# Attention scores in a Perceiver block: split fp32r products on the whole TensorE array, or full fp32 products on eight tiles of it

## The reference, cut to what matters

```python
q = (x @ Wq).reshape(B, N, H, D).transpose(0, 2, 1, 3)   # B 32, N 32, H 8, D 64
kv = (context @ Wkv).reshape(B, M, 2, H, D)              # M 257
k = kv[:, :, 0].transpose(0, 2, 1, 3)
v = kv[:, :, 1].transpose(0, 2, 1, 3)
q, k = _per_head_ln(q, qn_w), _per_head_ln(k, kn_w)
attn = jnp.einsum('bhnd,bhmd->bhnm', q, k) * SCALE       # the scores
attn = jnp.where(mask[:, None, :, :], attn, -jnp.inf)
attn = jax.nn.softmax(attn, axis=-1)
out = jnp.einsum('bhnm,bhmd->bhnd', attn, v)
```

## Time and profile before

| | |
|---|---|
| median of the three executions | 787.98 us |
| the profiled execution | 791.38 us |
| its span, first to last instruction | 789.6 us |
| mean granted clock of TensorE | 0.977 |
| PE busy, share of the span | 95% |
| steady batches, from 77 to 469 us | 392 us |

### The profile page before, as it was taken

One profiled execution on the slowest core, in us unless ns is written; L12 is line 12 of the kernel. 1 busy time (PEld: TensorE's weight loads), 2 busy tenths in 40 slices (PEclk: granted clock), 3 DMA queues, 4 the chain that ended last, 5 costly groups with the idle time before them and its releaser, 6 DMA issues.

```text
span 789.6 us, 13562 instructions
## 1 busy us (share of the span) xinstructions
PE 748.8 (95%) x4501; PEld 653.6 (83%) x4501; DVE 552.7 (70%) x1046; ACT 494.8 (63%) x1089; POOL 238.8 (30%) x182
## 2 busy tenths in 40 slices
PE   4898999999999999999999998999999958999996
PEld 3687899899999898998999997988788856877875
DVE  6877886776867868867868776885567754555573
ACT  4666786785867768767858666556465423655650
POOL 2562212121211212121212113842860002555545
PEclk9999999999999999999999999999999957999999
DMA  8841211212121211212121302661106472566658
GB/s 299 86 120 41 66 57 41 81 48 72 40 80 40 80 40 58 61 40 80 41 79 41 112 22 52 178 211 54 54 1 214 145 284 78 96 110 109 106 77 319
DMA packets 59671, 75.18 MB, mean 95 GB/s; under 512 B 8784, under 2 KB 33360, under 8 KB 59632
## 3 DMA queue, kind: packets, MB, share of 16 engines
q1 hardware_dynamic: 52032, 58.16, 24.8%
q0 software_dynamic: 4720, 11.27, 7.9%
q10 hardware_dynamic: 2880, 5.24, 1.8%
HBM read 54.75 MB, written 19.92 MB: 95 GB/s over the span
## 4 chain that ended last, share of the span: by engine, by line
PE 83%; DVE 7%; DMA 3%; ACT 3%; issue 2%; POOL 1%; SPq 0%; POOLq 0%; ACTq 0%; DVEq 0%
PE pK L32 38%; PE pV L32 14%; PE pP L32 11%; PE pS L32 6%; PE pT L1700 3%; PE pT L1519 3%; PE pP L1683 2%; DMA big<-x_rows,idx_x 1%; PE pT L1814 1%; DMA fin<-total 1%; PE pT L1499 1%; PE pS L1768 1%; DVE bst L976 1%; DMA total<-big,idx 1%; DVE head_mean L996 1%
## 5 line engine op out<-in xcount | busy, mean ns | idle before, releaser
L32 PE MATMUL pK<-parts 128*128 128x512 f32 x840 | 210.5, 398 | 0.7 <-POOL parts L547 0.7
L516 POOL TENSOR_TENSOR parts<-big,parts 128x1024 fp32r<-128x1024 f32 x32 | 77.3, 2416 | 338.8 <-ACT parts L741 338.8
L32 PEld LDWEIGHTS pK<-parts 128*128 128x128 f32 x840 | 152.3, 189 | 29.2 <-POOL parts L547 1.1
L32 PE MATMUL pK<-w,lhs 128*128 x276 | 71.5, 410 | 1.8 <-DVE lhs L1436 1.4
L32 PEld LDWEIGHTS pK<-w,lhs 128*128 128x128 f32 x276 | 51.9, 194 | 13.5 <-issue 3.5
L1018 DVE TENSOR_TENSOR kn<-pK,head_rs 128x512 f32<-128x512 f32 x62 | 42.6, 688 | 20.1 <-ACT head_rs L643 19.5
L1452 DVE TENSOR_TENSOR w_p<-big,w_p 128x1024 fp32r<-128x1024 f32 x22 | 27.0, 1226 | 39.5 <-ACT w_p L933 39.5
L769 ACT ACTIVATE pT<-pP 128x512 fp32r<-128x512 f32 x32 | 19.1, 598 | 55.6 <-PE pP L1683 55.6
L32 PE MATMUL pS<-kT,qblk 128*128 128x258 f32 x384 | 51.4, 284 | 2.0 <-DVE qoT L1052 2.0
L32 PE MATMUL pP<-pT,parts 128*128 128x256 f32 x384 | 53.0, 288 | 0.0
L32 PEld LDWEIGHTS pP<-pT,parts 128*128 128x128 f32 x384 | 47.6, 192 | 3.5
(11 more groups left out here) (320 smaller groups left out, 1638.2 us busy)
## 6 DMA issues: line engine op xcount, KB each, us to landing
big<-in_ctx_dram SPq DMA_DIRECT2D x32, 512.0 KB, 3.8
total<-zero SPq DMA_DIRECT2D x32, 256.0 KB, 4.0
w_raw<-in_L_ffn_w_dram SPq DMA_DIRECT2D x16, 512.0 KB, 5.6
big<-in_L_ffn_w_dram SPq DMA_DIRECT2D x8, 512.0 KB, 7.6
fin<-total SPq DMA_DIRECT2D x8, 512.0 KB, 7.2
big<-in_L_xattn_Wkv_dram SPq DMA_DIRECT2D x2, 1024.0 KB, 11.0
x_rows<-big ACTq DMA_DIRECT2D x8, 256.0 KB, 2.1
total<-big ACTq DMA_DIRECT2D x8, 256.0 KB, 2.4
```

The lines of the kernel that those rows point to most:

```text
L32: last = pe.matmul(out, lhs(a, c), rhs(b, c), start=start and c == first and n == 0, stop=stop and c == chunks - 1 and n == 2)
L516: nc.gpsimd.tensor_tensor(ctxN[:, u, LO], ctx_raw[:, u], ctxN[:, u, HI].bitcast(F32), ALU.subtract).then_inc(cn_lo, 1)
```

## The change

The queries and the keys of the scores are kept in fp32, unsplit. For each sequence POOL copies the queries into a compact tile `q_b` (one copy), ACT copies the keys of `pTT[0]` and DVE those of `pTT[1]` (one copy each). The scores of each head are one full fp32 product on a tile of the array of 64 rows by 32 columns, at `tile_position=(e * 64, c * 32)`: the stationary operand is the queries of the head (64 by 32), the moving operand its 257 keys. Head 2c+e writes rows 32c to 32c+31 of bank e, so the eight heads have eight different tiles. The order of the heads in the softmax tiles becomes (e, c), and `out_tile` reads its operands through `heads_of`, two pieces of 128 columns with a step between them. PE waits, ahead of the eight products, for five semaphores and a no-operation instruction. The zeroing of `qblk` and of a column of `kT` is dropped.

```diff
-        kT = at("kT", [P, 2, C, M + 1], 96 * KB, F32R)
-        qblk = at("qblk", [P, 2, 2, G, 3 * HD], 96 * KB + 8256, F32R)
+        kT = at("kT", [P, C, M], 96 * KB)
+        q_b = at("q_b", [P, 2, C, S], 96 * KB + 8256)
...
+        heads_of = lambda ap, c: ap.rearrange("p (e c) n -> p c e n", e=2)[:, c]
...
-            nc.gpsimd.memset(kT[:, :, :, M:M + 1].bitcast(F32), 0.0)
-            nc.gpsimd.memset(qblk[:, :, :, :, :].bitcast(F32), 0.0)
...
+            def queries(b, u, used=True):
+                if used:
+                    pool.wait_ge(sc_mm, b - 1)
+                nc.gpsimd.tensor_copy(q_b[:, u], qoT[:, :, bass.ds(b * S, S)]).then_inc(q_set, 1)
+
             ctx_parts(0, 0)
             low_part("xv", (2, 3))
+            pool.wait_ge(q_out, 1)
+            for b in range(2):
+                queries(b, b, used=False)
             ctx_parts(1, 1)
...
                 for u in range(2):
                     b = k * 2 + u
+                    queries(b, u)
                     ctx_parts(b, u)
...
+            def keys_copy(n):
+                act.wait_ge(k_t, (n - 1) * MT + 1)
+                act.activation(kT[:, :, 0:P], pTT[0][:, :, :], ACT.Copy).then_inc(kT0_set, 1)
...
                 if nxt:
-                    act.wait_ge(sc_mm, b)
-                    query_high(b + 1, 1 - u)
                     ctx_high(b + 1, 1 - u)
...
                 if main:
-                    for t in range(MT):
-                        act.wait_ge(k_t, b * MT + t + 1)
-                        act.activation(kT[:, HI, :, t * P:(t + 1) * P], pTT[t][:, :, :], ACT.Copy).then_inc(k_hi, 1)
+                    keys_copy(b + 1)
...
+            def keys_copy(n):
+                dve.wait_ge(k_t, n * MT)
+                ts(kT[:, :, P:MT * P], pTT[1][:, :, :], 1.0, None, ALU.mult).then_inc(kT1_set, 1)
...
                 if t == TILES - 1:
-                    query_low(1, 1)
+                    keys_copy(1)
                     dve.wait_ge(rem_act, 5)
-                    tt(kT_rem[:, LO], pAV[0][:, :, 0:B], kT_rem[:, HI].bitcast(F32), ALU.subtract).then_inc(rem_dve, 1)
-                    for n in range(MT):
-                        dve.wait_ge(k_hi, n + 1)
-                        tt(kT[:, LO, :, n * P:(n + 1) * P], pTT[n][:, :, :],
-                           kT[:, HI, :, n * P:(n + 1) * P].bitcast(F32), ALU.subtract).then_inc(k_lo, 1)
...
                 if nxt:
                     ctx_low(b + 1, 1 - u)
-                if nxt:
-                    query_low(b + 1, 1 - u)
...
                 if prev:
-                    pe.wait_ge(k_lo, b * MT)
-                    pe.wait_ge(qb_lo, b * 2)
+                    pe.wait_ge(kT0_set, b)
+                    pe.wait_ge(kT1_set, b)
                     pe.wait_ge(k_rem, b)
-                    for g in range(G):
-                        for j in range(2):
-                            c = 2 * g + j
-                            qb = lambda s, _: qblk[:, 1 - u, s, g, j * HD:j * HD + P]
-                            last = split_products(pe, pS[:, g, 0:M + 1], qb, lambda s, _: kT[:, s, c, :], 1,
-                                                  start=j == 0, stop=j == 1)
+                    pe.wait_ge(q_set, b)
+                    if not first:
+                        pe.wait_ge(sc_m, b - 1)
+                    pe.nop(nofuse=True)
+                    for c in range(C):
+                        for e in range(2):
+                            half = slice(e * HD, (e + 1) * HD)
+                            last = pe.matmul(pS[c * S:(c + 1) * S, e, 0:M], q_b[half, 1 - u, c, :],
+                                             kT[half, c, :], start=True, stop=True, tile_position=(e * HD, c * S))
                     last.then_inc(sc_mm, 1)
```

More of the change, by code:

```diff
@@ L164, in perceiver_block @@
         p_rem = at("p_rem", [P, G, 3, B], 117 * KB + 8320)
-        kT_rem = at("kT_rem", [P, 2, C, B], 118 * KB + 8064, F32R)
+        kT_rem = at("kT_rem", [P, C, B], 118 * KB + 8064)
         zero = at("zero", [P, P], 119 * KB + 8064)
@@ L265, in perceiver_block @@
         ctx_t, ctx_hi, ctx_lo = sem("ctx_t"), sem("ctx_hi"), sem("ctx_lo")
-        k_mm, k_sq, k_ss, k_lg, k_rs, k_n, k_t, k_hi, k_lo, k_rem = (sem(n) for n in (
-            "k_mm", "k_sq", "k_ss", "k_lg", "k_rs", "k_n", "k_t", "k_hi", "k_lo", "k_rem"))
+        k_mm, k_sq, k_ss, k_lg, k_rs, k_n, k_t, kT0_set, kT1_set, k_rem = (sem(n) for n in (
+            "k_mm", "k_sq", "k_ss", "k_lg", "k_rs", "k_n", "k_t", "kT0_set", "kT1_set", "k_rem"))
         cn_hi, cn_lo = sem("cn_hi"), sem("cn_lo")
         pc_mm, pc_hi, pc_lo = sem("pc_mm"), sem("pc_hi"), sem("pc_lo")
-        qb_hi, qb_lo, p_rs, p_rx, sel_set = (sem(n) for n in ("qb_hi", "qb_lo", "p_rs", "p_rx", "sel_set"))
+        q_set, p_rs, p_rx, sel_set = (sem(n) for n in ("q_set", "p_rs", "p_rx", "sel_set"))
         sc_mm, sc_m, sc_max, sc_exp, sc_step, p_n = (sem(n) for n in (
@@ L540, in _ @@
                     b = k * 2 + u
+                    queries(b, u)
                     ctx_parts(b, u)
-            ctx_parts(B - 2, 0)
-            ctx_parts(B - 1, 1)
+            for b in (B - 2, B - 1):
+                queries(b, b % 2)
+                ctx_parts(b, b % 2)
             def out_low(t):
@@ L662, in _ @@
             ln_scale(2)
-            def query_high(b, u):
-                for e in range(2):
-                    act.activation(q_half(b, u, HI, e), q_of(b, e), ACT.Copy).then_inc(qb_hi, 1)
             for t in range(TILES):
@@ L723, in _ @@
                     act.activation(head_rs[:, 2], head_log[:, 2], ACT.Exp, scale=-0.5).then_inc(k_rs, 1)
-                if t == 6:
-                    query_high(1, 1)
                 if t == TILES - 1:
@@ L728, in _ @@
                     act.wait_ge(rem_pe, 3)
-                    act.activation(kT_rem[:, HI], pAV[0][:, :, 0:B], ACT.Copy).then_inc(rem_act, 1)
-                    for n in range(MT):
-                        act.wait_ge(k_t, n + 1)
-                        act.activation(kT[:, HI, :, n * P:(n + 1) * P], pTT[n][:, :, :], ACT.Copy).then_inc(k_hi, 1)
+                    act.activation(kT_rem[:, :, :], pAV[0][:, :, 0:B], ACT.Copy).then_inc(rem_act, 1)
+                    keys_copy(1)
             k_square(1, 0)
@@ L1112, in _ @@
                 if t == TILES - 1:
-                    query_low(1, 1)
+                    keys_copy(1)
                     dve.wait_ge(rem_act, 5)
-                    tt(kT_rem[:, LO], pAV[0][:, :, 0:B], kT_rem[:, HI].bitcast(F32), ALU.subtract).then_inc(rem_dve, 1)
-                    for n in range(MT):
-                        dve.wait_ge(k_hi, n + 1)
-                        tt(kT[:, LO, :, n * P:(n + 1) * P], pTT[n][:, :, :],
-                           kT[:, HI, :, n * P:(n + 1) * P].bitcast(F32), ALU.subtract).then_inc(k_lo, 1)
-                    dve.wait_ge(rem_dve, 4)
-                    ts(kT[:, :, :, M - 1:M], kT_rem[:, :, :, 0:1].bitcast(F32), 1.0, None, ALU.mult).then_inc(k_rem, 1)
+                    ts(kT[:, :, M - 1:M], kT_rem[:, :, 0:1], 1.0, None, ALU.mult).then_inc(k_rem, 1)
             query_out(TILES - 1)
@@ L1188, in batch @@
                     dve.wait_ge(k_t, b * MT + 1)
[L1189 to L1193, removed]
+                    ts(kT[:, :, M - 1:M], kT_rem[:, :, bass.ds(b, 1)], 1.0, None, ALU.mult).then_inc(k_rem, 1)
+                    keys_copy(b + 1)
                 if main and not nxt:
@@ L1605, in out_tile @@
                     split_products(pe, o, lambda s, k: wkv[:, s, k, D + c * P:D + (c + 1) * P],
-                                   lambda s, k: z_p[:, s, k, c * 2 * P:(c + 1) * 2 * P], C, stop=False)
+                                   lambda s, k: heads_of(z_p[:, s, k].rearrange("p (h n) -> p h n", h=H), c), C, stop=False)
                     if c == 0:
@@ L1609, in out_tile @@
                     last = pe.matmul(o, vrem[0:3 * B, c * P:(c + 1) * P],
-                                     rem_b[0:3 * B, 2 * c:2 * c + 2].rearrange("p h b q -> p (h b q)"), start=False, stop=True)
+                                     heads_of(rem_b[0:3 * B].rearrange("p h b q -> p h (b q)"), c), start=False, stop=True)
                     if c % 2:
@@ L1675, in batch @@
                     if first:
-                        pe.wait_ge(rem_dve, 4)
+                        pe.wait_ge(rem_act, 5)
                     else:
@@ L1710, in batch @@
                                 if first:
-                                    pe.wait_ge(rem_dve, 5)
+                                    pe.wait_ge(rem_dve, 4)
                                 elif r == 0:
```

8 lines of the change are left out of this document (removed).

## The result

The changed kernel takes 766.85 us (median of four, 766.68 to 767.52) against 788.31 us for the kernel before in the same comparison: 21.5 us less, a ratio of 0.973 with a 95% interval of 0.9713 to 0.9747. The forecast was faster by 3.8 us, with a range that ended at 770: the side was right, the size was not, and the result lies outside the range.

A forecast was written before the change was run, and what follows sets the result against it. PE was taken to bound the loop: 2.9 us saved in the scores over 32 sequences and 0.9 us once at the start, 788.0 - 3.8 = 784.2 us; own range 770 to 793, for all cases 770 to 816.

The forecast's parts named there:

- The new waits: PE's added waits for the score copy, key copies and query copies: all met ahead of need, costing nothing.
- The start: Chain through DVE ahead of the first scores: they start near 63.4 in place of 64.34, saving 0.9 us once.
- The two ends: Entering and leaving the tiled shape on PE: 0 to 0.56 us together, taken at the middle, 0.28 us.
- the emptied array: Rival: PE empties at both shape changes around the scores, paying the full 0.56 us; 793 us, chance 0.13.
- the body of X: PE time of the sixteen tile passes of a sequence's scores, without the entry and exit cost: 1.07 us.
- X: PE time from scores' start to transposes' start: 1.35 us, range 0.9 to 1.63, against 1.44 before; 2.9 us saved.
- 14 issues at 0.05 us: Score passes limited by issue: last tile's first pass starts at 0.70 us, the scores' passes take 1.12 us.
- five passes in a row: Each half of the rows works its four tiles in order, neighbouring tiles' passes overlapping: 5 x 0.213 = 1.07 us.
- The lower end: Bound for the score passes on PE: all eight tiles at once, two passes, 2 x 0.213 = 0.43 us.
- One order for all tiles: Rival: score matmuls start in program order, only one pass overlapping the next tile's; X 2.2 us, 811 us, chance 0.21.
- no overlap: Rival: the score tiles run one after the other, X 3.7 us; 859 us, chance 0.09.
- The hidden gain: Rival: PE's scores get shorter, but PE then waits for the probabilities; 787 us, chance 0.07.

The follow-up runs named there:

- the work put back: Changed kernel with copies and subtractions into unused memory on ACT and DVE, about the work they had lost: 768.0 us, ratio 0.9736.
- the run with the halves apart: Changed kernel with the four tiles of the upper half of the rows issued first, then the four of the lower half: 767.52 us, ratio 0.9742.
- the run with each head twice: Changed kernel with each head's product issued twice in a row on its tile, same output: 781.53 us, ratio 0.9904.

## Why the prediction was wrong in size

**Right.** PE alone bounds the loop, and everything of ACT, DVE and POOL in it is under its cover: the work put back cost nothing in the loop. The new waits cost nothing. The start was worth 0.94 us where 0.9 was said. The length of a pass, 0.213 us by columns, was 0.21 to 0.22. The two ends were taken at 0.28 us out of 0 to 0.56 and are about 0.24; that the middle came so close is luck, since it was a choice between two bounds. No change of shape was free, and none cost the full 0.56, so the emptied array (793 us) did not come true as priced. Whether the array is emptied for part of that price, no row tells: the first tile matmul starts at 307.37, 0.07 us ahead of the modelled end of the last full one.

**The step that failed** is the body of X: "I take 1.07, near the lower end". It is 0.50 us: two passes of 0.24 and 0.22 and 0.05 for the starts. In place of 14 issues at 0.05 us or five passes in a row, all eight tiles ran beside each other. The lower end of 0.43 that the prediction had written down ("all eight tiles at once, two passes") was the right mechanism; I gave it no weight, drew the forecast's own range only down to X of 0.9, for which there was no row, and named no sign for an X below it. The term cost (1.07 - 0.50) x 32 = 18 us, against 17.3 us between forecast and result. The ends, 0.24 in place of 0.28, gave 1.3 us more; the steps that saved 0.675 in place of 0.70 took 0.8 back, the wait for the probabilities 0.5 and the longer wait for POOL behind the 32nd scores 0.7.

Both intermediate ways behind the 1.07 were wrong. The price of issue, 0.05 us a pair, came from eight bf16 products, and that stretch ran at half the granted clock, while the loop runs at 1.00 (same columns as above):

```profile
637.90:639.00 1.10, 0.50 (x9) 0.42 (x9) 0.96 (x7) 1.09 (x2) 0.00 (x0) 0.50 1.05 395
```

That is at most a factor of two. The tile products leave 0.007 us apart, eight within 0.06 us, a seventh of 0.05; so what set the spacing of the bf16 products, each with a load of 128 columns, was not issue. And no half of the rows works its tiles in order, as the run with the halves apart shows.

**The rivals.** One order for all tiles (811 us, a chance of 0.21) and no overlap (859 us, 0.09) are refuted by the starts, and the first also by the run with each head twice, whose scores would have been 25 passes in a row, 25 x 0.213 = 5.3 us, and took 1.07. The page of the Trainium skill whose rule spoke for one order ("TensorE: Matmul & The Clock Gate", Part 3, "What overlaps and what doesn't") does not hold for these products: eight first passes are in flight by 307.43 and no second one until 307.60, and with each head twice even the second product of tile 1 starts behind the first of tile 8. The hidden gain (0.07) is real only in the last step, where the wait for the probabilities took 0.5 us.

The ends of a visit cost 0.2 to 0.25 us here. The Trainium skill ("TensorEngine Tiling (Array Packing)", "Key Properties") says that changing the tiling mode drains the engine, and gives no price. The prediction had worked out 0.56 us for a full drain at both ends; the trace shows under half of that.

## What to carry to other kernels

The full fp32 products of this kernel on disjoint tiles cost the passes of the busiest tile plus about 0.24 us for a visit, with 8 or 16 products, on two tiles or eight, and nearly whatever their order; so put all of them into one visit and spread them evenly. Before choosing between a split product and a full fp32 one, count passes on the busiest tile: here 12 passes in a row (1.44 us) lost to two (0.74 us with the ends), while the same full products on the whole array took 1.74 us. When a resource is new to the kernel, bound it by the rows, but don't centre the forecast on a price taken from rows that measure something else, and look at the granted clock of the stretch that a price is read from.

## What the runs showed of the hardware that was not expected

- A backlog on one tile does not hold up the others: with four passes per tile issued in a row, the eight first passes were still all in flight within 0.16 us, ahead of every second pass.
- Eight tile products started within 0.06 us, 0.007 us apart, while a full-array pass of the same width takes 0.217 us.
- A pass on a tile of 64 rows by 32 columns takes as long as on the whole array (0.21 to 0.22 us for 257 columns), so a tile gains by company alone.
- Entering and leaving the tiled shape cost 0.2 to 0.25 us a visit together; 0.08 us of it shows ahead of the tiles (1.45 us in place of 1.37) and 0.06 us behind them (0.85 in place of 0.79).
- Behind PE's waits ahead of the last scores (2.0 and 0.5 us in the changed kernel) the granted clock fell to 0.50 for 3.4 us in nine of the twelve profiled executions and stayed at 1.00 in three, which alone made 1.5 us between two executions with the same scores.
